# Attention output: gate parts made during the heads, gate products one group ahead, norm by pairs on ScalarE

## The chip, the cores and the metric

The kernel runs on 1 core of one Trainium2 chip. The metric is the device time of one execution in microseconds (us), and the comparison goes by the median of several runs. Engines: PE (TensorE, with its weight load PEld), DVE (VectorE), ACT (ScalarE), POOL (GpSimd) and SP (SyncE, which here only issues DMAs). Each engine has its own instruction stream and the streams meet by semaphores alone.

## What is computed

Two layers, each of an attention-like mixer and a feed-forward part, over x of 8 x 256 tokens with 512 features (2048 tokens). The change lies in the last part of the second mixer ("L1_xattn"); cut to it:

```python
O  = einsum('hst,bthe->bshe', A, V).reshape(b, s, dim)      # the D heads, four of them
mu = O.mean(-1);  var = O.var(-1)
Y  = (O - mu) / sqrt(var + 1e-3) * gn_gamma + gn_beta
W  = relu(x @ wg_w)                                          # x: layer norm of the stream
x  = x + (W * Y) @ wo_w
# next: h = layernorm(x), router and LoRA parts, 44 chunks of the second feed-forward part
```

All of it is in float32, made of float32r parts: a matrix is cut into a high part (a copy in fp32r) and a low part (the matrix minus that copy), and a product is three matmuls: high x high, low x high, high x low (helper `product`, L313 to L317).

## The kernel before

Everything is written out by hand: one function for each engine with its instructions in order, and `wait_ge` on semaphores. The 2048 tokens are 16 tiles of 128, in 4 groups of 4. The eight PSUM banks hold 512 float32 columns each.

**The D heads.** `heads` (L324) runs four heads in the order second(h), first(h+1), weigh(h). On PE, first projects two token groups of the context, second makes the scores and projects the other two, and weigh multiplies the floored scores A with V (24 matmuls of 512 columns). POOL makes the low parts of the context, `low(h, q)` (L529 to L532, tile ccl), in a loop; the projection of group q waits for them. DVE makes |A| (L1565), its floor at 1 (L1567), the low parts of x (xxl, L1541) and of A (al, L1571), and copies half of the results out (ret, L1612). ACT makes the high parts (cch, xxh, ah) and copies the other half (L780). The arrays ct (context) and xt (x, turned so that features lie on partitions) stay in SBUF for the whole stage.

**The output stage.** When all heads are done (`END_D`), `gated` (L349) runs over the four groups: `turned_and_gate(0)`, then `turned_and_gate(g)` and `out_rows(g-1)` in a loop of two, then the rest. For a group:
- DVE: statistics of four tiles (`ln_stats`, L286 to L294), POOL the power -0.5 (L551), DVE applies the norm to four tiles (xn, L299).
- PE turns the four tiles of xn into banks 0 to 3 (L310), ACT scales and shifts them into zt (L804, 16 instructions).
- ACT and POOL make the parts of x of this group, xeh (L789) and xel (L559, one instruction of 2048 columns); PE makes the gate product x @ Wg in banks 4 to 7 (48 matmuls of 512 columns); DVE takes the relu out of PSUM and multiplies it into zt (L1642).
- ACT and DVE cut zt into uh (L821) and ul (L1634); PE multiplies by Wo into banks 0 to 3 (48 matmuls), DVE adds the result to xres (L1656).

The weights' parts wgh, wgl, woh, wol are made once at the start of this stage: high parts on ACT (L793, L796), low parts on DVE (L1627, L1629). The norm of the feed-forward part then goes by pairs of tiles: `pair(n)` on DVE (L1390 to L1398), `pair_root(n)` on POOL (L525, L527), `apply(n)` on ACT (L669), `turn_f` on PE. The last `out_rows` is interleaved with it.

**SP** loads wgf and wof behind the last low part of the context (L403, L404), five small tensors behind `END_D` (L406 to L409), and the first two chunk weights `wst` when the weights' low parts are made (L413).

Of the kernel before, what the change touches and what calls it, by code (L numbers as in the profile page):

```python
# [53 lines left out]
def build(nc, x, ctx_in, taps, d_heads, consts, bits, rw, rb, ew, eb, wh, decay, wg, wo, gb,  # L54
# [15 lines left out]
    with stack:  # L70
# [21 lines left out]
        def place(spot, *buffers):  # L92
# [60 lines left out]
        wgf, wof, wgh, wgl, woh, wol, xeh, xel = place(  # L153
            CT_AT, ("wgf", [P, KB, DIM], F32), ("wof", [P, KB, DIM], F32), ("wgh", [P, KB, DIM], F32R),
            ("wgl", [P, KB, DIM], F32R), ("woh", [P, KB, DIM], F32R), ("wol", [P, KB, DIM], F32R),
            ("xeh", [P, KB, GTOK], F32R), ("xel", [P, KB, GTOK], F32R))
        zt, uh, ul, gbc = place(
            W_AT + 1024, ("zt", [P, KB, GTOK], F32), ("uh", [P, KB, GTOK], F32R), ("ul", [P, KB, GTOK], F32R),
            ("gbc", [P, 2 * KB], F32))

# [31 lines left out]

        def turned(t, tile):
            return t[:, :].rearrange("p (k n) -> p k n", k=KB)[:, :, bass.ts(tile, P)]
# [19 lines left out]
        ln = {st: {k: sem(f"{st}_{k}", 1 if k == "xn" else 0) for k in ("stats", "var", "rstd", "xn")} for st in "AE"}  # L214
# [32 lines left out]
        wg_in, wo_in, wE_high, wE_ready = sem("wg_in"), sem("wo_in"), sem("wE_high"), sem("wE_ready")  # L247
        xeh_ready, xel_ready, wt_done = sem("xeh_ready"), sem("xel_ready"), sem("wt_done", 1)
        y_turned, zt_ready, zu_ready, uh_ready = sem("y_turned", GROUP), sem("zt_ready"), sem("zu_ready", 1), sem("uh_ready")
        ul_ready, wo_done, x3_ready = sem("ul_ready", 1), sem("wo_done", GROUP), sem("x3_ready", GROUP)  # L250
# [89 lines left out]
        END_E = [(x3_ready, TILES)]  # L340
# [5 lines left out]

        EARLY = 1

        def gated(eng, start, turned_and_gate, out_rows):  # L349

            start()
            turned_and_gate(0, True)
            with eng.Fori(1, GROUPS - 1, 1) as g:
                turned_and_gate(g, True)
                out_rows(g - 1)
            turned_and_gate(GROUPS - 1, False)
            out_rows(GROUPS - 2)
            out_rows(GROUPS - 1)
# [13 lines left out]
        def _(sp):  # L372
# [42 lines left out]
            sp.wait_ge(wE_ready, 2)  # L415
# [58 lines left out]
        def _(pool):  # L474
# [74 lines left out]
            def rstd_e(g):  # L549
                pool.wait_ge(ln["E"]["var"], g + 1)  # L550
                pool.tensor_tensor(rstd[:, :], vare[:, 0, :], mhalf[:, :], ALU.pow).then_inc(ln["E"]["rstd"], 1)  # L551

            def nothing(g):
                pass

            def low_xe(g):
                pool.wait_ge(xeh_ready, g + 1)
                pool.sem_inc(passed, 1)
                pool.tensor_tensor(xel[:, :, :], turned_group(xt, g), f(xeh[:, :, :]), ALU.subtract)\  # L559
                    .then_inc(xel_ready, 1)  # L560

            def start():
                rstd_e(0)
                low_xe(0)

            def prepare(g, more):
                if more:
                    rstd_e(g + 1)
                    low_xe(g + 1)

            gated(pool, start, prepare, nothing)
# [4 lines left out]
            for n in range(TILES, TILES + TILES // 2):  # L576
                pair_root(n)
# [24 lines left out]
        def _(act):  # L602
# [59 lines left out]
            def apply(n):  # L662

                act.wait_ge(pair_rstd, n + 1)
                for i in (2 * n, 2 * n + 1):
                    j = i % GROUP
                    if i >= GROUP:
                        act.wait_ge(xn_turned, i - GROUP + 1)
                    act.activation(xn[:, j, :], xres[:, i % TILES, :], ACT.Identity,  # L669
                                   bias=nmr[:, j:j + 1], scale=rstd[:, j:j + 1]).then_inc(xn_ready, 1)  # L670
# [101 lines left out]

            def weigh(h):
# [10 lines left out]
            after(act, END_D)  # L784

            def high_x(g):
                act.wait_ge(wt_done, raised(wt_done) + KB * g)
                act.sem_inc(passed, 1)
                act.activation(xeh[:, :, :], turned_group(xt, g), ACT.Copy).then_inc(xeh_ready, 1)  # L789

            def start():
                act.wait_ge(wg_in, 16)
                act.activation(wgh[:, :, :], wgf[:, :, :], ACT.Copy).then_inc(wE_high, 1)  # L793
                high_x(0)
                act.wait_ge(wo_in, 32)
                act.activation(woh[:, :, :], wof[:, :, :], ACT.Copy).then_inc(wE_high, 1)  # L796

# [1093 lines left out]
```

## Time and profile before

| | |
|---|---|
| runs | 1153.96, 1159.79, 1159.83 us, median 1159.79 |
| the profiled execution | 1154.15 us, span 1152.3 us |
| mean granted clock of TensorE | 0.972 of full |
| busy: PE, PEld, DVE, ACT, POOL | 93%, 75%, 54%, 38%, 51% |

A profile is one execution. Its page gives busy shares and the chain of work that ended last. The views of the trace cut the span into stretches (busy time of each engine and the clock that TensorE was granted, 1.00 being 2.4 GHz and 0.50 being 1.2 GHz) or list instructions in order of time, each with its start and duration and, in brackets, the idle time of its engine just ahead of it and what ended that. Equal instructions in a row are merged ("x4"). A matmul's duration holds its way through the array, so matmuls that follow each other overlap; the distance of their starts is what counts. The D heads run from about 342 to 431 us, the output stage from there to about 549.

### The profile page before, as it was taken

What the parts mean: (1) busy time and instruction counts of PE and PEld (TensorE: products, weight loads), DVE (VectorE), ACT (ScalarE), POOL (GpSimd) and SP (SyncE); (2) the same over time, 40 slices, a digit from 0 to 9 for tenths busy, and PEclk for the clock granted to TensorE, in tenths of its full rate; (3) what the DMA queues carried; (4) which work ended last, traced back from release to release, by engine and by line L of the source; (5) the groups of instructions that cost most, each with busy time, mean ns of one, the idle gap of its engine ahead of it and who ended that gap; (6) DMA issues with size and microseconds to landing.
All of it is one profiled execution on the core that took longest, in us unless ns stands there. A gap on an engine that the chain in (4) does not pass through costs nothing.

```text
span 1152.3 us, 13470 instructions
## 1 busy us (share of the span) xinstructions
PE 1068.2 (93%) x4924; PEld 863.7 (75%) x4924; DVE 624.1 (54%) x1046; ACT 440.6 (38%) x803; POOL 588.8 (51%) x402
## 2 busy tenths in 40 slices
PE   5799998588889985999999999999999999999997
PEld 4577776465568864778668888888888888888886
DVE  6399999846875637756552352423424244242223
ACT  5354444441184535443532332333332232233222
POOL 1588996120032203230227676766776677667662
PEclk9899999888999988999999999999999999999999
DMA  8222121000010012000322212252323432232211
GB/s 306 92 55 64 56 56 28 1 1 1 1 37 1 1 74 97 1 1 1 165 89 87 96 69 87 78 185 105 116 74 107 155 132 80 95 113 87 71 67 37
DMA packets 24560, 85.47 MB, mean 74 GB/s; under 512 B 3169, under 2 KB 3825, under 8 KB 23729
## 3 DMA queue, kind: packets, MB, share of 16 engines
q1 hardware_dynamic: 22384, 80.45, 20.6%
q10 hardware_dynamic: 2112, 4.19, 1.0%
q8 instruction: 38, 0.62, 0.2%
q14 instruction: 26, 0.20, 0.1%
HBM read 74.85 MB, written 9.78 MB: 73 GB/s over the span
## 4 chain that ended last, share of the span: by engine, by line
PE 73%; DVE 19%; issue 4%; ACT 2%; POOL 1%; POOLq 0%; DVEq 0%; ACTq 0%
PE banks L315 23%; PE banks L316 22%; PE banks L317 22%; DVE qt L1372 6%; DVE pr L1366 6%; PE banks L310 3%; DVE pr L1368 1%; DVE stat L1390 1%; DVE junk L1466 1%; PE banks L939 1%; ACT xn L669 1%; PE banks L993 1%; PE banks L1187 0%; DVE xn L299 0%; DVE xtl L1402 0%
## 5 line engine op out<-in xcount | busy, mean ns | idle before, releaser
L1774 DVE TENSOR_TENSOR hf<-banks,silu 128x512 f32<-128x512 f32 x132 | 91.3, 692 | 323.5 <-PE banks L317 322.2
L582 POOL TENSOR_TENSOR gul<-wst,guh 128x1280 fp32r<-128x1280 f32 x44 | 129.9, 2952 | 141.7 <-DVE guh L1672 135.8
L592 POOL TENSOR_TENSOR hl<-hf,hh 128x512 fp32r<-128x512 f32 x129 | 178.2, 1412 | 8.6 <-ACT hh L897 8.6
L939 PE MATMUL banks<-kv,strip 128*128 128x288 f32 x640 | 158.4, 412 | 4.1 <-POOL kv L491 4.1
L897 ACT ACTIVATE hh<-hf 128x512 fp32r<-128x512 f32 x132 | 83.6, 633 | 190.0 <-DVE hf L1774 190.0
L939 PEld LDWEIGHTS banks<-kv,strip 128*128 128x128 f32 x640 | 123.4, 193 | 39.0 <-issue 4.4
L895 ACT ACTIVATE silu<-banks 128x512 f32<-128x512 f32 x132 | 78.9, 598 | 167.4 <-PE banks L317 167.2
L315 PE MATMUL banks<-xf,guh 128*128 128x512 f32 x352 | 137.2, 390 | 0.8 <-POOL gul L582 0.8
L316 PE MATMUL banks<-xf,guh 128*128 128x512 f32 x352 | 137.0, 389 | 0.0
L317 PE MATMUL banks<-xf,gul 128*128 128x512 f32 x352 | 136.9, 389 | 0.0
L525 POOL TENSOR_TENSOR rstd<-vare,mhalf 128x2 f32<-128x2 f32 x24 | 20.2, 842 | 150.7 <-DVE vare L1398 150.7
L587 POOL TENSOR_TENSOR dnl<-wst,dnh 128x640 fp32r<-128x640 f32 x44 | 68.9, 1566 | 42.6 <-DVE dnh L1769 42.6
L315 PEld LDWEIGHTS banks<-xf,guh 128*128 128x128 f32 x352 | 66.1, 188 | 15.8 <-POOL gul L582 1.3
L317 PEld LDWEIGHTS banks<-xf,gul 128*128 128x128 f32 x352 | 66.1, 188 | 13.7
L316 PEld LDWEIGHTS banks<-xf,guh 128*128 128x128 f32 x352 | 66.1, 188 | 13.5
L1366 DVE TENSOR_TENSOR pr<-banks,qx 128x1024 f32<-128x1024 f32 x32 | 65.2, 2038 | 16.5 <-ACT yx L643 15.8
L1372 DVE TENSOR_REDUCE qt<-pr 128x256 f32<-128x2048 f32 x32 | 73.2, 2286 | 1.1
L502 POOL TENSOR_TENSOR pr<-yx,qx 128x768 f32<-128x768 f32 x32 | 59.7, 1866 | 27.0 <-ACT yx L643 21.0
L310 PE MATMUL banks<-cst,xn 128*128 128x128 f32 x320 | 50.0, 304 | 24.9 <-DVE xn L299 12.3
L315 PE MATMUL banks<-rhl,guh 128*128 128x512 f32 x176 | 68.7, 390 | 0.4 <-ACT silu L895 0.3
L315 PE MATMUL banks<-dnh,hh 128*128 128x512 f32 x176 | 68.8, 391 | 0.0
L317 PE MATMUL banks<-rhl,gul 128*128 128x512 f32 x176 | 68.5, 389 | 0.0
(281 smaller groups left out, 2284.3 us busy)
## 6 DMA issues: line engine op xcount, KB each, us to landing
wst<-in_chunk_w SPq DMA_DIRECT2D x44, 960.0 KB, 4.7
strip<-toep SPq DMA_DIRECT2D x32, 256.0 KB, 3.2
xres<-in_x ACTq DMA_DIRECT2D x4, 1024.0 KB, 13.1
cin<-in_ctx SPq DMA_DIRECT2D x16, 256.0 KB, 5.7
xf_s<-xf SPq DMA_DIRECT2D x2, 2048.0 KB, 6.3
out<-xres SPq DMA_DIRECT2D x16, 256.0 KB, 2.1
xf<-xf_s SPq DMA_DIRECT2D x8, 512.0 KB, 5.9
mk<-hot_s SPq DMA_DIRECT2D x14, 256.0 KB
```

What stands on the lines that cost most here:

```text
L310: i = pe.transpose(banks[:, bank, k * P:(k + 1) * P], src[:, k, :], ident)
L315: pe.matmul(dst, wh_, mh_, start=first, stop=False, skip_group_check=check)
L316: pe.matmul(dst, wh_, ml_, start=False, stop=False, skip_group_check=check)
L317: return pe.matmul(dst, wl_, mh_, start=False, stop=last, skip_group_check=check)
L582: pool.tensor_tensor(gul[:, u, :], wst[:, u, 0:GU_W], f(guh[:, u, :]), ALU.subtract).then_inc(gul_ready, 1)
L592: pool.tensor_tensor(hl[:, u, s, :], hf[:, s, :], f(hh[:, u, s, :]), ALU.subtract)\
L895: act.activation(silu[:, s % 2, :], banks[:, 6, :], ACT.Silu).then_inc(silu_done, 1)
L897: act.activation(hh[:, u, s, :], hf[:, s, :], ACT.Copy).then_inc(hh_ready, 1)
L939: mm = pe.matmul(dst, strip[:, h % 3, far:far + P], view(kv, h % 3, m * BATCH * PAIRS, [[PAIRS, BATCH], [1, PAIRS]]), start=m == 0, stop=m ...
L1366: dve.tensor_tensor(view(pr, u, 0, [[HD * HD, MB], [1, 4], [HD, HD]]), rows, view(qx, u, 0, [[2 * HD, MB], [1, 4], [1, HD]]), ALU.mult)
L1372: dve.tensor_reduce(head_cols(qt, h), view(pr, u, 0, [[HD * HD, MB], [HD, HD], [1, HD]]), X_AXIS, ALU.add).then_inc(conv_out, 1)
L1774: dve.tensor_tensor(hf[:, s, :], banks[:, 7, :], silu[:, s % 2, :], ALU.mult).then_inc(mul_done, 1)
```

## The change

- **Weights' parts.** Wg is loaded once ct's first head is used. POOL copies it to wgh in four pieces in head 2 and subtracts to wgl in four pieces in head 3. Wo's high part is made by ACT in four pieces, its low part by POOL in four pieces, one behind each of the first four `pair_root`. Its load wof now lies on zt's place, and the first scaling waits for its low parts.
- **x parts.** They are made in pieces of 512 columns, `high_xe(g, k)` on ACT and `low_xe(g, k)` on POOL. Group 0's are made in the heads, groups 1 and 2 around the last weigh, group 3 behind the second scaling. The low parts overwrite xt.
- **Gate products.** PE runs gate(0) ahead of the last weigh, and then gate(1), turn(0), gate(2), turn(1), out(0), gate(3), turn(2), out(1), turn(3), out(2), out(3). ACT copies each gate bank to SBUF (`keep_w`, 16 copies), so DVE's relu and product read SBUF twice.
- **Norm.** The group norm of Y goes by pairs like the norm that follows (pair indices move up by 8): statistics on DVE, roots and -mean x root on POOL, application on ACT.
- The loops are written out. The first chunk weights are loaded behind the first low part of xf.

The core of the diff:

```diff
+        def xel(g, k):
+            return xtr[:, k * TOKENS + g * GTOK:k * TOKENS + (g + 1) * GTOK]
...
-            sp.wait_ge(ccl_ready, 4 * RHEADS)
+            sp.wait_ge(ccl_ready, 4)
             sp.dma_start(wgf[:, :, :], wg).then_inc(wg_in, 16)
+            for u in range(2):
+                sp.wait_ge(sc_done[u], raised(sc_done[u]) + 2 * RHEADS)
             sp.dma_start(wof[:, :, :], wo).then_inc(wo_in, 16)
             after(sp, END_D)
-            sp.dma_start(gbc[:, :], gb).then_inc(wo_in, 16)
+            sp.dma_start(gbc[:, :], gb).then_inc(lw_in, 16)
...
-            sp.wait_ge(wE_ready, 2)
+            sp.wait_ge(xfl_ready, 1)
             load(0, 0, 0)
...
-            with pool.Fori(1, RHEADS, 1) as h:
-                for q in range(4):
-                    low(h, q)
-            after(pool, END_D)
...
+            def low_xe(g, k):
+                pool.wait_ge(xeh_ready, KB * g + k + 1)
+                pool.wait_ge(xxl_ready, 4 * k + g + 1)
+                pool.tensor_tensor(xel(g, k), xt_part(g, k), f(xe[g][:, k, :]), ALU.subtract).then_inc(xel_ready, 1)
+
+            for h in range(1, RHEADS):
+                low(h, 0)
+                low(h, 1)
+                if h == 1:
+                    low_xe(0, 0)
+                if h == 2:
+                    pool.wait_ge(wg_in, 16)
+                    for k in range(KB):
+                        pool.tensor_copy(wgh[:, k, :], wgf[:, k, :]).then_inc(wgh_ready, 1)
+                    low_xe(0, 1)
+                if h == 3:
+                    for k in range(KB):
+                        pool.wait_ge(wgh_ready, k + 1)
+                        pool.tensor_tensor(wgl[:, k, :], wgf[:, k, :], f(wgh[:, k, :]), ALU.subtract).then_inc(wgl_ready, 1)
+                    low_xe(0, 2)
+                low(h, 2)
+                low(h, 3)
+            low_xe(0, 3)
+            for g in (1, 2):
+                for k in range(KB):
+                    low_xe(g, k)
+            for n in range(TILES, TILES + TILES // 2):
+                pair_root(n)
+                if n < TILES + KB:
+                    k = n - TILES
+                    pool.wait_ge(woh_ready, k + 1)
+                    pool.tensor_tensor(wol[:, k, :], wof[:, k, :], f(woh[:, k, :]), ALU.subtract).then_inc(wol_ready, 1)
+                if n == TILES + KB + 1:
+                    for k in range(KB):
+                        low_xe(3, k)
...
+            def keep_w(g, jb):
+                act.wait_ge(wt_done, KB * g + jb + 1)
+                if g >= 2:
+                    act.wait_ge(zu_ready, KB * (g - 2) + KB)
+                act.activation(wk[g % 2][:, jb, :], banks[:, W_BANKS[g][jb], :], ACT.Copy).then_inc(wr_ready, 1)
+
             def weigh(h):
                 if h == RHEADS - 1:
+                    act.wait_ge(mv_done[0], raised(mv_done[0]) + 2 * RHEADS)
+                    act.wait_ge(mv_done[1], raised(mv_done[1]) + 2 * RHEADS)
+                    for k in range(KB):
+                        high_xe(1, k)
                     act.wait_ge(a_ready, h + 1)
                     act.activation(ah[:, :], aw[:, :], ACT.Copy).then_inc(ah_ready, 1)
+                    for k in range(KB):
+                        high_xe(2, k)
+                    for jb in range(KB):
+                        keep_w(0, jb)
...
+                if h < 2:
+                    if h == 0:
+                        act.wait_ge(xn_turned, 2 * TILES)
+                    high_xe(0, 2 * h)
+                    high_xe(0, 2 * h + 1)
...
+            def scaled(g):
+
+                if g == 0:
+                    act.wait_ge(wol_ready, KB)
+                    act.wait_ge(lw_in, 80)
+                else:
+                    act.wait_ge(ul_ready, GROUP * g)
...
+            apply(TILES)
+            keep_w(1, 0)
+            apply(TILES + 1)
+            keep_w(1, 1)
+            keep_w(1, 2)
+            keep_w(1, 3)
+            scaled(0)
+            apply(TILES + 2)
+            keep_w(2, 0)
+            apply(TILES + 3)
+            keep_w(2, 1)
+            high_u(0)
+            keep_w(2, 2)
+            keep_w(2, 3)
+            scaled(1)
+            apply(TILES + 4)
+            apply(TILES + 5)
+            for k in range(KB):
+                high_xe(3, k)
...
+            high_u(1)
+            for jb in range(KB):
+                keep_w(3, jb)
+            scaled(2)
+            apply(TILES + 6)
+            apply(TILES + 7)
+            high_u(2)
+            scaled(3)
+            high_u(3)
...
+            def weigh_last(h):
+                if h == RHEADS - 1:
+                    gate(0)
+                weigh(h)
+
+            heads(pe, start, first, second, weigh_last)
...
+            gate(1)
+            turn_y(0)
+            gate(2)
+            turn_y(1)
+            out_rows(0)
+            gate(3)
+            turn_y(2)
+            out_rows(1)
+            turn_y(3)
+            out_rows(2)
+            out_rows(3)
...
+            def gated_features(g):
+                for jb in range(KB):
+                    dve.wait_ge(wr_ready, KB * g + jb + 1)
+                    dve.wait_ge(zt_ready, GROUP * g + GROUP)
+                    dve.scalar_tensor_tensor(zt[:, jb, :], wk[g % 2][:, jb, :], 0.0, zt[:, jb, :], ALU.max, ALU.mult)\
+                        .then_inc(zu_ready, 1)
...
+            for n in range(4):
+                pair(TILES + n)
+            gated_features(0)
+            for j in range(GROUP):
+                low_u(0, j)
+            pair(TILES + 4)
+            pair(TILES + 5)
+            gated_features(1)
+            out_rows(0)
+            pair(TILES + 6)
+            pair(TILES + 7)
+            gated_features(2)
+            out_rows(1)
+            gated_features(3)
+            out_rows(2)
+            out_rows(3)
```

## Rows read from the trace of the kernel before

**Rows 1.** The page: busy time by engine (us, share, instructions), and the chain's shares.

```profile
PE 1068.2 (93%) x4924; PEld 863.7 (75%) x4924; DVE 624.1 (54%) x1046; ACT 440.6 (38%) x803; POOL 588.8 (51%) x402
PE 73%; DVE 19%; issue 4%; ACT 2%; POOL 1%; POOLq 0%; DVEq 0%; ACTq 0%
```

**Rows 2.** Stretches: length, busy (count) PE, PEld, DVE, ACT, POOL, PEclk, DMA, GB/s.

```profile
418.94:523.40 104.46, 84.60 (x375) 69.89 (x375) 67.43 (x95) 44.48 (x87) 26.80 (x10) 0.90 0.08 27
```

**Rows 3.** Timeline, PE, output stage: start, duration, instruction, [idle before, what ended it].

```profile
422.41 0.79 PE L315 MATMUL banks<-vh,ah 128*128 128x512 f32 x1 [3.47 <-DVE al L1571]
...
441.17 3.65 PE L310 MATMUL banks<-cst,xn 128*128 128x128 f32 x16 [10.27 <-DVE xn L299]
...
463.03 0.79 PE L315 MATMUL banks<-xeh,wgh 128*128 128x512 f32 x1 [5.11 <-POOL xel L559]
...
523.86 0.39 PE L315 MATMUL banks<-woh,uh 128*128 128x512 f32 x1
```

**Rows 4.** Timeline, PE: the end of a gate product and a turn.

```profile
455.78 0.39 PE L317 MATMUL banks<-xeh,wgl 128*128 128x512 f32 x1
456.01 1.91 PE L310 MATMUL banks<-cst,xn 128*128 128x128 f32 x16
```

**Rows 5.** Timeline, DVE: the norm's applications of groups 0 and 1.

```profile
436.31 6.09 DVE L299 TENSOR_SCALAR xn<-ret,mom,rstd 128x512 f32<-128x512 f32 x4 [1.22 <-POOL rstd L551]
...
451.04 1.92 DVE L299 TENSOR_SCALAR xn<-ret,mom,rstd 128x512 f32<-128x512 f32 x4 [1.12 <-POOL rstd L551]
```

**Rows 6.** Timeline, DVE and ACT: prices of a pair, a copy, a scaling, a cast.

```profile
536.21 1.28 DVE L1390 BATCH_NORM_STATS2 stat<-xres 128x6 f32<-128x512 f32 x2
...
539.12 1.52 ACT L669 ACTIVATE xn<-xres,nmr,rstd 128x512 f32<-128x512 f32 x2 [3.56 <-POOL nmr L527]
...
429.67 0.60 ACT L780 ACTIVATE ret<-banks 128x512 f32<-128x512 f32 x1 [3.61 <-PE banks L317]
...
442.36 5.69 ACT L804 ACTIVATE zt<-banks,gbc 128x128 f32<-128x128 f32 x16 [5.02 <-PE banks L310]
...
599.76 0.82 DVE L1672 CAST guh<-wst 128x1280 fp32r<-128x1280 f32 x1
```

**Rows 7.** Landing time of the wgf load; timeline, DVE: first reader of wst.

```profile
DMA to landing us min/median/max: 4.9/4.9/4.9
...
568.39 0.82 DVE L1683 CAST guh<-wst 128x1280 fp32r<-128x1280 f32 x1
```

**Rows 8.** Timeline, POOL, DVE and PE ahead of weigh(2), in the D heads.

```profile
396.67 2.55 POOL L531 TENSOR_TENSOR ccl<-ct,cch 128x512 fp32r<-128x512 f32 x2 [6.88 <-ACT cch L714]
...
399.14 0.69 DVE L1565 SCALAR_TENSOR_TENSOR aw<-aw 128x512 f32<-128x512 f32 x1
...
401.41 0.69 DVE L1571 TENSOR_TENSOR al<-aw,ah 128x512 fp32r<-128x512 f32 x1
...
402.15 0.50 PE L315 MATMUL banks<-vh,ah 128*128 128x512 f32 x1
```

**Rows 9.** Timeline, POOL and PE, head 1: context low parts and their reader.

```profile
366.58 2.53 POOL L531 TENSOR_TENSOR ccl<-ct,cch 128x512 fp32r<-128x512 f32 x2 [8.71 <-ACT cch L714]
...
370.47 0.40 PE L315 MATMUL banks<-cch,grh 128*128 128x512 f32 x1
```

**Rows 10.** Timeline, DVE and POOL: two-input DVE instructions beside POOL's.

```profile
664.42 1.45 DVE L1739 TENSOR_TENSOR rf<-ra,mk 128x512 f32<-128x512 f32 x1
665.80 1.78 DVE L1740 TENSOR_TENSOR rf<-ra,mk 128x512 f32<-128x512 f32 x1
667.50 0.68 DVE L1739 TENSOR_TENSOR rf<-ra,mk 128x512 f32<-128x512 f32 x1
...
665.28 1.74 POOL L592 TENSOR_TENSOR hl<-hf,hh 128x512 fp32r<-128x512 f32 x1
```

**Rows 11.** Stretches as in rows 2: after the 3.47 idle, and a head change.

```profile
422.40:428.40 6.00, 5.99 (x14) 4.73 (x15) 0.35 (x1) 0.60 (x1) 0.00 (x0) 0.50 0.00 0
...
367.00:372.00 5.00, 4.48 (x35) 4.38 (x36) 2.36 (x5) 2.17 (x5) 2.11 (x2) 1.00 0.00 0
```

More of the change, by code:

```diff
@@ L151, in build @@
             ("xxh", [P, 2, GTOK], F32R), ("xxl", [P, 2, GTOK], F32R))
[L153 to L156, printed above, removed]
+        wgf, = place(CT_AT, ("wgf", [P, KB, DIM], F32))
+        wgh, wgl = place(CT_AT + 8192, ("wgh", [P, KB, DIM], F32R), ("wgl", [P, KB, DIM], F32R))
+        wr0, = place(CT_AT, ("wr0", [P, KB, GTOK], F32))
+        wr1, woh, wol, xe1, xe2 = place(
+            CT_AT + 24576, ("wr1", [P, KB, GTOK], F32), ("woh", [P, KB, DIM], F32R), ("wol", [P, KB, DIM], F32R),
+            ("xe1", [P, KB, GTOK], F32R), ("xe2", [P, KB, GTOK], F32R))
+        xe0, = place(BASE + 34816, ("xe0", [P, KB, GTOK], F32R))
+        wof, = place(W_AT + 1024, ("wof", [P, KB, DIM], F32))
         zt, uh, ul, gbc = place(
@@ L781, in weigh @@
                                    banks[:, bank, :].rearrange("p (b e) -> p b e", b=4), ACT.Copy).then_inc(ro_act, 1)
-            heads(act, start, first, second, weigh)
[L784 to L796, printed above, removed]
-            def scaled(g, more):
-                act.wait_ge(ul_ready, raised(ul_ready) + GROUP * g)
+                if h < 2:
[3 more added lines that the diff above has]
+                    high_xe(0, 2 * h + 1)
+            heads(act, start, first, second, weigh)
+            act.wait_ge(ao_done, raised(ao_done) + 4 * RHEADS)
+            act.wait_ge(wo_in, 16)
+            for k in range(KB):
+                act.activation(woh[:, k, :], wof[:, k, :], ACT.Copy).then_inc(woh_ready, 1)
+            def scaled(g):
[4 more added lines that the diff above has]
+                    act.wait_ge(ul_ready, GROUP * g)
                 for j in range(GROUP):
-                    act.wait_ge(y_turned, raised(y_turned) + GROUP * g + j + 1)
+                    act.wait_ge(xn_turned, 2 * TILES + GROUP * g + j + 1)
                     for k in range(KB):
@@ L827, in _ @@
-            gated(act, start, scaled, out_rows)
+            apply(TILES)
[15 more added lines that the diff above has]
+            apply(TILES + 5)
@@ L857, in _ @@
             keep_a(0, 0)
-            apply(TILES + 5)
+            apply(TILES + 13)
             high_f(8)
@@ L1132, in weigh, with gate @@
                     mm.then_inc(ao_done, 1)
-            heads(pe, start, first, second, weigh)
-            after(pe, END_D)
-            def turned_and_gate(g, more):
+            def gate(g):
+                pe.wait_ge(wgl_ready, KB)
+                pe.wait_ge(xel_ready, KB * g + KB)
+                for jb in range(KB):
+                    if g == 0 and jb >= 2:
+                        pe.wait_ge(vl_ready[jb - 2], raised(vl_ready[jb - 2]) + 2 * RHEADS)
+                    if g == 1 and jb == 1:
+                        pe.wait_ge(ro_act, raised(ro_act) + 2 * RHEADS)
+                        pe.wait_ge(ro_vec, raised(ro_vec) + 2 * RHEADS)
+                    if g >= 2:
+                        pe.wait_ge(wr_ready, KB * (g - 1) + jb + 1)
+                    for k in range(KB):
+                        mm = product(pe, banks[:, W_BANKS[g][jb], :], wgh[:, k, jb * P:(jb + 1) * P],
+                                     wgl[:, k, jb * P:(jb + 1) * P], xe[g][:, k, :], xel(g, k), k == 0, k == KB - 1)
+                    mm.then_inc(wt_done, 1)
@@ L1672, in cut_gu @@
                 dve.tensor_copy(guh[:, u, :], wst[:, u, 0:GU_W]).then_inc(guh_ready, 1)
-            gated(dve, start, gated_features, out_rows)
+            for n in range(4):
[14 more added lines that the diff above has]
+            out_rows(3)
             for n in range(4, TILES // 2):
-                pair(TILES + n)
+                pair(TILES + 8 + n)
                 low_f(2 * n - 4)
```

168 lines of the change are left out of this document (61 added, 107 removed).

## The prediction

> **What bounds the kernel now.** I read the page's busy times and chain first: PE is busy for 93% of the span and the chain that ended last is 73% PE [rows 1]. So the kernel is a TensorE kernel, and a change to helpers is worth only what PE idle time or half-clock time it removes. The stretch table then shows where that time is [rows 2]: from the end of the D heads' scores (418.94, 3.47 ahead of the matmul at 422.41) to the first out-projection matmul of group 2 (523.86 [rows 3]) PE is busy 84.6 us of 104.5 and its granted clock is 0.90. The work in this stretch, at full clock: a 512-column matmul comes every 0.227 us (455.78 to 456.01, rounded) and 16 transposes take 1.91, the last overlapping what follows, 1.75 from start to start [rows 4]. Weigh of the last head is 24 matmuls (5.4 us), four gate products are 192 (43.5), two out-projections are 96 (21.8), four turns are 7.0: 77.7 us. The stretch is 104.9, so **27.2 us** are idle or slow. They are, in order [rows 3]: 3.5 idle before weigh(3) and then 24 matmuls until 430.9, 8.3 instead of 5.4 (2.9 more); 10.3 idle before the first turn of Y, and that turn in 3.5 instead of 1.75 with a slow start of the gate (2.3 in all); 5.1 idle until xel of group 1 exists, then 1.3 at half clock; the last 1.8 are waits of some tenths. What ends the 10.3 is a chain of DVE and POOL work: statistics of four tiles, the POOL power, and four xn applies that took 6.09 us where four later ones took 1.92, because POOL's xel ran beside them [rows 5].
>
> **Gain in the output stage.** (Times below are those of before, as if the D heads kept their time.)
> 1. gate(0) moves in front of weigh(3): its inputs (Wg parts, x parts of group 0) are made in the D heads. PE runs it from 418.94 to 429.8, weigh(3) to 435.3, gate(1) to 446.2, turn_y(0) to 448.1, gate(2) to 459.0, turn_y(1) to 460.9, all without a pause if ACT keeps up. The old cover of DVE's floor(3) was none; it is now 10.9 us.
> 2. The norm by pairs: pair(16) starts when the last ret copy is through, 436.4. A pair takes 2.9 us from its first statistic to ACT's start, of which I put 1.8 on DVE and 1.0 on POOL, and 1.5 on ACT for two tiles [rows 6]. POOL does a wol piece (1.27) behind each of four roots, and pair n+2 waits for apply n. The wol pieces end at 440.6, 442.9, 445.2 and 447.5.
> 3. **The wait added**: scaled(0) waits for all four wol pieces, since zt lies on wof: it starts at 447.5, not at its first turned tile. Queued behind it on ACT are two applies, four keeps of the gate, four uh copies and scaled(1). With 5.69 for a scaled, 1.52 for an apply of two, 0.6 for a keep or a uh [rows 6], scaled(1) starts at 447.5 + 5.7 + 1.5 + 0.6 + 1.5 + 0.6 + 2.4 + 1.2 = 461.0 and gives its first tile at 462.4. PE waits for it with out_rows(0) from 460.9: 1.5 us. POOL's pieces can push DVE's small pair instructions and so this chain by some 1 more: 2.5.
> 4. Group 3's x parts: high_xe(3) comes behind scaled(1) and two applies, POOL needs 4 x 1.27 for them, so they are complete 14.4 us after scaled(1) starts; PE is through out_rows(0) 12.4 after it. Stall 2.0 to 2.6, taken as 2.3. Before out_rows(1) and out_rows(2) PE waits for the first tile of scaled(2) and (3): 0.5 and 1.0.
> 5. Sum of stalls left: 6.3, and one spell at half clock, 1.7 (about as after the 5.1 gap). **27.2 - 8.0 = 19.2 us** gained in this stage. Bounds: 22 without contention and slow spells; 14 with every POOL piece in the way once and two slow spells.
> The two spare moves cost nothing. SP's wof load now waits for the last scores; it is issued near 419, the equal load of wgf lands in 4.9 us [rows 7], and woh needs it at 434. Nothing stands behind it on SP until the heads end. The five small loads behind it are issued 4.5 us later than now and are needed at 447.5. The first wst loads move behind the first xf part, near 535; their first reader stands at 568.39 [rows 7], so over 20 us of cover remain. The tail from out_rows(3) on is the same work in the same order.
>
> **Cost in the D heads.** POOL gets 4 copies of Wg and one low_xe in the middle of head 2, 4 subtractions and one low_xe in head 3. All lie in POOL's queue behind low(h,1) and ahead of low(h,2), and start the moment low(h,1) ends: 399.22 in the old times of head 3 [rows 8]. POOL has 8.7 us of idle time before low(h,2) [rows 9], so low(h,2) isn't late; nor is head 1, where the two ACT copies and low_xe(0,0) make ccl 1.3 + 1.3 late against 370.47, the first project that reads it (366.58 + 1.3 now, 369.2 then [rows 9]). But look what DVE does in those 5 us [rows 8]: |A|, floor, two xxl, and al, and al ends at 402.10 where weigh starts at 402.15. There is no slack. DVE instructions that read two SBUF tensors, and the copies and scalings from SBUF to SBUF, do not run beside a POOL tensor instruction in this trace: the xn applies lost 4.2 us to xel [rows 5]; two rf in a row, each 0.68 alone, took 1.45 and 1.78 beside two hl of POOL, and the second of these (665.28, 1.74 instead of 1.29) let the first rf through and then held up the second [rows 10]. So they take turns, even when DVE's instructions stand back to back. |A| is in when POOL starts (399.14); then floor, xxl, xxl and al each wait for one POOL piece: **al is late by four pieces**, and weigh with it. In head 3 a piece is a subtraction, 1.26: 5.0 us. In head 2 it is a one-input copy that no row of POOL shows. High end: the two-input row, 1.26, so 5.0. Low end: DVE's own one-input cast takes 0.82 for 1280 columns and its two-input subtraction 0.69 for 512 [rows 6, 8], half per column, so 0.65 and 2.6. I take the low end, as the nearest in kind. Sum 7.6, at most 10.0; nothing if the claims don't collide at all.
> The clock: the gap of 3.5 at 418.94 was followed by 5.7 us at 0.50; the gap of 1.0 at every head change leaves 1.00 [rows 11]. Half clock costs half of its time. A gap of 5.0 should bring 1.7 to 3.4, one of 2.6 brings 0 to 3.4: I take 3.4 together. **Cost 11.0 us.**
> The Trainium skill, "SBUF — State Buffer", section "SBUF: two separate sides", says that DVE and GpSimd share a port pair as an exclusive lock held for the whole instruction, for DVE instructions with two SBUF inputs or in a two-port mode. The rf rows agree; by that rule ACT's applies, which the change puts in the place of DVE's, never wait. "GPSIMD Engine Reference", section 4.1, calls one-input work on GpSimd roughly line rate; that would make the copy about 0.45 and the estimate for head 2 1.8 instead of 2.6. No run here shows it.
>
> **Sum.** 19.2 - 11.0 = 8.2 us. Against the profiled execution: its time is 1154.15 (span 1152.3), so 1146.0. The runs shown are 1153.96, 1159.79 and 1159.83; the profiled one is of the lower kind, 5.6 under the median, and 8.2 off the median is 1151.6. I forecast 1149, between the two.
>
> **Rivals.**
> *The port claims don't matter in the heads* (POOL's pieces slip into the holes, or PE's own queue hides al). For it: POOL is 8 us idle there. Against: al ends 0.05 ahead of weigh, and the rf rows. Then 19.2 are kept: 1135 on the profile's basis, 1140 on the median's. Chance 0.17.
> *A draw*: copies at 1.26 each, slow clock after both gaps (3.4 each), output stage at its low end: 14 - 10.0 - 6.8 = -2.8; with one of the slow spells missing it is +0.6. For it: POOL rows are all at 1.26 for this shape. 1153 to 1162. Chance 0.24.
> *Slower*: |A| loses the tie with POOL's first piece (it starts 0.08 ahead of low(h,1)'s end now) so al waits for five pieces in both heads: 12.6, clock 6.8; and low_xe(3) and wol, made in the output stage, hold gated and ul there. These now read SBUF on both sides, where gated read PSUM, so each of the 8 in a POOL burst can lose 1.3. This costs 10 beyond the stalls above: 19.2 - 19.4 - 10 = -10. With the fifth piece and both slow spells in place, the sign turns at the first held instruction, and 0.5% is passed at the fifth. 1164 to 1170. Chance 0.09.
> *It doesn't do what it says* (gate(0) starts late, since Wg's low parts come last on POOL): against, they are issued 15 us ahead of 418.94. It is in the draw's chance.
>
> **How the numbers follow.** Main forecast 0.50. Within it the gain runs from about 2 to 14 us. A measurement of this kernel can tell about 0.5% (5.8 us) from no change. Faster by more: three quarters of the main case plus nearly the whole first rival, and a little of it lost to which kind of run the median falls on: 0.56. Within 0.5%: the rest of the main case and most of the draw: 0.31. Slower: the third rival and a part of the draw: 0.13. The range goes from the first rival on the profile's basis to the draw's upper part: 1136 to 1161.
>
> **What would show it.** PE without a gap at 418.94 and clock 1.00 there; turn_y(0) right behind gate(1). In heads 2 and 3 a PE gap of 2.6 and of 5.0 ahead of weigh(1) and weigh(2), al late, DVE's xxl at 1.3 to 1.9 instead of 0.69 and POOL pieces stretched by 0.4 to 0.6. POOL's Wg copies at 0.65, not 1.3. ACT's scaled(0) starting where the fourth wol ends. The forecast is wrong if PE runs through weigh(1) and weigh(2) as now, or if gated and ul in the output stage take over 1 us each.

## The result, and the profile after

Nine runs of each kernel on one chip: before 1152.72 us (1151.57 to 1159.83), after **1145.81 us** (1145.11 to 1148.22), ratio after to before 0.9934, with a 95% interval of 0.9915 to 0.9953. So the change gains 6.9 us, 0.6%; the forecast was 1149, from a sum of 8.2. The profiled execution after is the 1145.11 one.

The page: busy time by engine, and the shares of the chain [rows 1 for before].

```profile
span 1143.3 us, 13422 instructions
...
PE 1065.9 (93%) x4924; PEld 861.4 (75%) x4924; DVE 607.7 (53%) x1040; ACT 459.1 (40%) x849; POOL 608.9 (53%) x438
...
PE 71%; DVE 20%; issue 4%; ACT 3%; POOL 1%; POOLq 0%; DVEq 0%; ACTq 0%
```

The shares hardly move: work went from DVE to ACT and POOL, and PE is still the bound. What moved shows in two places.

**The output stage.** Stretches (length, busy of PE, PEld, DVE, ACT, POOL, PEclk, DMA, GB/s) from the end of the scores of head 3 to the first out-projection of group 2, then right behind PE's two long gaps in the D heads [rows 2, 11 for before]:

```profile
426.85:511.64 84.79, 78.58 (x377) 65.17 (x376) 41.42 (x86) 54.95 (x114) 30.09 (x33) 1.00 0.07 22
...
381.50:385.50 4.00, 4.00 (x12) 3.15 (x12) 0.76 (x2) 0.60 (x1) 0.00 (x0) 0.63 0.00 0
409.00:412.50 3.50, 3.50 (x11) 2.71 (x11) 0.73 (x2) 0.60 (x1) 0.00 (x0) 0.60 0.00 0
```

104.9 us have become 84.8, **20.1 less** (forecast 19.2), and the clock in them is 1.00. PE is busy 78.6 of the 84.8; the prediction counted 77.7 of work. The rest, 6.2, is what PE waits for. PE's waits from 374 to 535 us (total, times, longest):

```profile
PE banks L330 <- DVE al L1651: 7.5, 2, 5.1
PE banks L330 <- ACT zt L834: 4.3, 3, 2.6
PE banks L330 <- DVE ret L1692: 2.0, 2, 1.0
PE banks L330 <- issue: 1.9, 1, 1.9
PE banks L325 <- DVE xf L1727: 0.2, 1, 0.2
```

The second and fourth lines are the stage's four stalls: 4.3 + 1.9 = 6.2. The fourth is put down to "issue", but it ends with the parts of x of group 3: POOL's last piece of them ends at 483.99, PE's gate(3) starts at 484.09.

**The D heads.** The first line is new: PE waits for the low part of A twice, 7.5 us. Here is head 3, the timeline of DVE, POOL and PE (start, duration, instruction, idle before and what ended it) [rows 8 for before]:

```profile
399.62 0.69 DVE L1642 TENSOR_TENSOR aw<-banks,dmask 128x512 f32<-128x512 f32 x1 [1.72 <-PE banks L332]
400.34 1.75 DVE L1645 SCALAR_TENSOR_TENSOR aw<-aw 128x512 f32<-128x512 f32 x1
402.13 1.39 DVE L1647 TENSOR_SCALAR aw<-aw 128x512 f32<-128x512 f32 x1
403.44 3.42 DVE L1621 TENSOR_TENSOR xxl<-xt,xxh 128x512 fp32r<-128x512 f32 x2
406.78 1.74 DVE L1651 TENSOR_TENSOR al<-aw,ah 128x512 fp32r<-128x512 f32 x1
```

```profile
400.27 6.04 POOL L567 TENSOR_TENSOR wgl<-wgf,wgh 128x512 fp32r<-128x512 f32 x4
406.27 1.70 POOL L552 TENSOR_TENSOR xtr<-xt,xe 128x512 fp32r<-128x512 f32 x1
```

```profile
408.58 0.80 PE L330 MATMUL banks<-vh,ah 128*128 128x512 f32 x1 [5.09 <-DVE al L1651]
```

Five POOL pieces and five DVE instructions go through each other, one of the one, one of the other: each xxl takes 1.7 instead of 0.64, POOL's piece 1.5 instead of 1.26. al is late and PE stands for 5.09 us. From the last ret copy of one head to that of the next there are 20.7 us in an undisturbed head; head 2 has 24.8 and head 3 27.4 (+4.1, +6.7 = **10.8**, forecast 11.0).

**The account.** The profiled spans differ by 9.0. Of that 3.0 is there before head 2: POOL's last ccl of head 1 starts at 375.99 before and at 372.97 after. The change did little there that could help; such offsets of 1 to 3 us come and go between all the kernels below, with the places of PE's half-clock spells in the 370 us ahead. What follows that instruction I call **the tail**: it is the cleanest part of a profile to compare. Before 776.3, after 770.3, 6.0 less: about 20.1 won in the stage, 10.8 lost in the heads, and 3.1 lost in two half-clock spells of after, from 555 and from 1135 on, which before does not have. Each lasts 3.4 us. What one costs is read by taking the same matmul, counted from the end of the program, in both profiles: after falls back by 1.6 over the first spell and by 1.5 over the second. Both come behind a wait of PE that before has as well, at full clock (1.53 us before the first, 2.77 before the second).

### The profile page after: what moved, and what is told of

Read it like the earlier page. It is cut to its first block, busy times and chain, and to the rows that moved or that the text cites. A ratio compares the mean times of both kernels' runs of the same rounds, so it can differ in the third digit from the quotient of the medians.

```text
span 1143.3 us, 13422 instructions
## 1 busy us (share of the span) xinstructions
PE 1065.9 (93%) x4924; PEld 861.4 (75%) x4924; DVE 607.7 (53%) x1040; ACT 459.1 (40%) x849; POOL 608.9 (53%) x438
## 4 chain that ended last, share of the span: by engine, by line
PE 71%; DVE 20%; issue 4%; ACT 3%; POOL 1%; POOLq 0%; DVEq 0%; ACTq 0%
PE banks L330 22%; PE banks L331 21%; PE banks L332 21%; DVE qt L1450 6%; DVE pr L1444 6%; PE banks L325 2%; DVE pr L1446 1%; DVE stat L1469 1%; ACT xn L682 1%; DVE junk L1546 1%; ACT zt L834 1%; PE banks L1265 1%; PE banks L989 1%; PE banks L1043 1%; DVE xxl L1621 0%
## 5 line engine op out<-in xcount | busy, mean ns | idle before, releaser
L529 POOL TENSOR_TENSOR rstd<-vare,mhalf 128x2 f32<-128x2 f32 x32 | 25.8, 806 | 184.1 <-DVE vare L1478 184.1
L332 PEld LDWEIGHTS banks<-xf,gul 128*128 128x128 f32 x352 | 66.1, 188 | 13.8
L330 PE MATMUL banks<-rhl,guh 128*128 128x512 f32 x176 | 68.8, 391 | 0.4 <-ACT silu L945 0.3
L331 PE MATMUL banks<-rhl,guh 128*128 128x512 f32 x176 | 68.6, 390 | 0.0
L332 PE MATMUL banks<-dnh,hl 128*128 128x512 f32 x176 | 68.5, 389 | 0.0
```

Of the source, the lines that this page charges most:

```text
L330: pe.matmul(dst, wh_, mh_, start=first, stop=False, skip_group_check=check)
L331: pe.matmul(dst, wh_, ml_, start=False, stop=False, skip_group_check=check)
L332: return pe.matmul(dst, wl_, mh_, start=False, stop=last, skip_group_check=check)
```

## The experiments

Two theories stood against each other. **Turns**: POOL's pieces and DVE's chain to al hold each other up, and the whole cost of the heads goes if the pieces come behind al. **Load**: the heads cost because POOL, ACT and DVE have more to do in them, wherever the pieces stand. All ratios are against runs of the kernel before on the same chip. Its medians in these groups lie between 1152.65 and 1153.06, so medians of different groups can be set side by side to within some tenths. Tails are of the profiled executions.

| kernel | median us | ratio, 95% interval | tail us |
|---|---|---|---|
| e1_behind_al | 1132.19 | 0.9819 [0.9803, 0.9835] | 756.5 |
| e2_head2_only | 1140.30 | 0.9887 [0.9869, 0.9905] | 763.6 |
| e3_before_pieces | 1162.34 | 1.0076 [1.0058, 1.0095] | 786.8 |
| e7_before_pieces_al | 1152.86 | 0.9999 [0.9990, 1.0009] | 776.6 |
| e4_gate0_late | 1149.43 | 0.9978 [0.9965, 0.9991] | 773.8 |
| e9_al_gate0 | 1139.36 | 0.9876 [0.9853, 0.9899] | 763.3 |
| e5_act_order | 1132.72 | 0.9825 [0.9801, 0.9848] | 757.0 |
| e6_apply_dve | 1133.67 | 0.9827 [0.9804, 0.9851] | 756.9 |
| e8_he_first | 1133.48 | 0.9825 [0.9802, 0.9848] | 756.3 |
| e10_uh_early | 1129.24 | 0.9787 [0.9772, 0.9802] | 753.1 |

### The pieces behind al, in both heads and in one

```diff
                 if h == 2:
+                    pool.wait_ge(al_ready, raised(al_ready) + h)
                     pool.wait_ge(wg_in, 16)
...
                 if h == 3:
+                    pool.wait_ge(al_ready, raised(al_ready) + h)
```

> The changed kernel (1145.8 us median), but in heads 2 and 3 POOL waits for al of the head before ahead of its Wg copies, Wg subtractions and low_xe. Nothing else moves. Theory (turns at the port between DVE and POOL): al is back in time, the PE gaps of 2.43 and 5.09 us ahead of weigh(1) and weigh(2) go, and the slow spells behind them (1.7 and 1.6 us) with them: 10.8 us less, about 1135. POOL has 5 pieces of 0.65 to 1.3 us and 5.8 us until the next low part, so that may be late by under 1 us, hidden by 2.5 us until its reader. Rival (the gaps come from something else that the change brought into the heads, such as ACT's extra copies): no change, 1144 to 1147.

Measured 1132.19, 13.6 under the changed kernel; the tail is 13.8 shorter, for 10.8 of the heads and 3.1 of the two late spells, which e1 does not have. DVE, POOL of e1 in head 2:

```profile
378.56 1.28 DVE L1623 TENSOR_TENSOR xxl<-xt,xxh 128x512 fp32r<-128x512 f32 x2
379.76 0.68 DVE L1653 TENSOR_TENSOR al<-aw,ah 128x512 fp32r<-128x512 f32 x1
```

```profile
380.51 2.29 POOL L563 CAST wgh<-wgf 128x512 fp32r<-128x512 f32 x4 [3.05 <-DVE al L1653]
382.76 1.29 POOL L552 TENSOR_TENSOR xtr<-xt,xe 128x512 fp32r<-128x512 f32 x1
```

Each xxl is back at 0.64 and al at 0.68, PE has no wait for al in either head, and the pieces still end in time: the very same work, started 3.1 us later. The load theory falls. The copy by itself is seen here: 2.29 for four, 0.57 each.

e2_head2_only has the first of the two waits alone.

> As the run before it, but only head 2's pieces wait for al; head 3's stay where the change put them. Theory: 4.1 us less than the changed kernel (gap 2.43 and 1.7 of half clock), about 1141.7; head 3 keeps its gap of 5.09. Rival (the cost is that of any POOL burst of this length, or the clock alone): the difference is not in the proportion of 4.1 to 6.7.

1140.30; PE waits for al once, 5.1. The step from e2 to e1 (head 3) is 8.1, in the tails 7.1; the stretch of head 3 in the changed kernel had said 6.7, and 0.4 more is lost there in e2, since less of its half-clock spell lies under PE's gap. From after to e2 (head 2) it is 5.5, in the tails 6.7, of which 4.1 are the head and 3.1 the two late half-clock spells, absent here too, less the same 0.4. Why they are gone was not tried.

### The pieces put into the kernel before

Ten POOL instructions of the same shape, on ct and into the idle xn, behind low(2,1) and low(3,1) of the kernel before, which has none of the rest of the change.

```diff
+            for h in range(1, RHEADS):
+                low(h, 0)
+                low(h, 1)
+                if h > 1:
+                    for i in range(4):
+                        piece(h == 2)
+                    piece(False)
+                low(h, 2)
+                low(h, 3)
```

> The kernel before, and only POOL work added: four copies of 128x512 and one subtraction behind low(2,1), four subtractions and one more behind low(3,1), all into the tile of xn, which is free in the heads; nobody reads them. It prices the cost in the heads by itself. Theory: 10.8 us slower than before, 1163.5 on a median of 1152.7, with gaps of 2.4 and 5.1 us ahead of weigh(1) and weigh(2). Rival (the gaps in the changed kernel come from its waits and ACT copies): no slower.

1162.34, +9.6 on the median of before beside it; the tail is 10.5 longer, PE waits for al twice, 2.21 and 3.94. The second was expected at 5.1. These subtractions read the same tensor twice and take 1.04 alone (in e7), not 1.26, and each link of DVE's chain is late by 0.83 to 0.85 at a piece, where the changed kernel has 1.06; the floor is late by 0.72. In head 3 of this kernel (timeline of DVE):

```profile
403.99 2.97 DVE L1563 TENSOR_TENSOR xxl<-xt,xxh 128x512 fp32r<-128x512 f32 x2
406.88 1.52 DVE L1593 TENSOR_TENSOR al<-aw,ah 128x512 fp32r<-128x512 f32 x1
```

e7_before_pieces_al is the same with one more line, `pool.wait_ge(al_ready, raised(al_ready) + h)`, ahead of the pieces.

> The same ten POOL pieces in the kernel before, but each burst waits for al of the head before. Theory: the same POOL work costs nothing there, 1152 to 1154: what costs is where it stands against DVE's chain. Rival (POOL's work in itself is the price, by delaying its own low parts): 2 to 10 us slower.

1152.86, ratio 0.9999, tail 0.3 longer: the same ten instructions cost nothing behind al. POOL's five subtractions of head 3, alone here:

```profile
400.91 5.04 POOL L556 TENSOR_TENSOR xn<-ct 128x512 f32<-128x512 f32 x5 [3.06 <-DVE al L1595]
```

With e1 this settles the heads from both sides: it is the place, not the work.

### gate(0) in front of the last weigh

```diff
             def weigh_last(h):
+                weigh(h)
                 if h == RHEADS - 1:
                     gate(0)
-                weigh(h)
```

with ACT's `keep_w(0, *)` behind woh.

> The changed kernel (1145.8) with one part undone: gate(0) stands behind weigh(3) on PE instead of ahead of it (and its four copies on ACT behind the last ret copies). Theory (gate(0) is the cover of DVE's and ACT's work on A of the last head): PE stands idle from the last scores to al, 5.5 us in the changed kernel's times, and then runs at half clock for 3.4 to 6.8 us; 7.2 to 8.9 us slower, 1153 to 1155. Rival (the norm's chain is what had to be covered, and two gates behind weigh cover it just as well): within 1 us of the changed kernel, since gate(0) and gate(1) are then both behind the last ret copies.

1149.43, only 3.6 over the changed kernel, where 7 to 9 were expected. PE does wait (5.4 once more for al, and half clock behind it), yet the profile of e4 lacks the two late spells of after. The rows say 5.4 + 1.9 (half clock, by e9 below) - 0.7 (waits for zt of 3.6 instead of 4.3) = 6.6; less 3.1 for the two spells is 3.5, and the tails say 3.5. So the same edit was tried on e1, which has no late spells to lose.

> e1_behind_al with gate(0) behind weigh(3) instead of in front, and its four keep copies on ScalarE behind woh: the same edit as in e4_gate0_late, on a kernel whose D heads lose nothing. Theory (gate(0) in front covers floor(3) to al(3) on DVE, a PE gap of 5.4 us in e4_gate0_late at the end of the scores, with a half-clock spell behind it of 1.7 to 3.4 lost, and 4.5 of that is won back since the statistics of Y start earlier in front of gate(1) and PE's waits for scaled are shorter by 0.7): slower than e1_behind_al by 5 to 8, so 1137 to 1140. Rival (the place of gate(0) is worth only what e4_gate0_late showed against the changed kernel, 3.6 us, whatever the heads do): 1135 to 1136.5. The trace should show one PE wait for al of about 5.4 at the end of the scores and half clock behind it.

1139.36, **7.2** over e1, tails 6.8. PE's gap in e9, the stretch behind it, and what DVE does ahead of it:

```profile
423.11 0.80 PE L330 MATMUL banks<-vh,ah 128*128 128x512 f32 x1 [5.45 <-DVE al L1653]
```

```profile
423.20:427.50 4.30, 4.30 (x11) 3.42 (x12) 0.00 (x0) 1.81 (x4) 4.30 (x4) 0.56 0.00 0
```

```profile
418.54 1.73 DVE L1647 SCALAR_TENSOR_TENSOR aw<-aw 128x512 f32<-128x512 f32 x1
420.30 1.37 DVE L1649 TENSOR_SCALAR aw<-aw 128x512 f32<-128x512 f32 x1
422.36 0.69 DVE L1653 TENSOR_TENSOR al<-aw,ah 128x512 fp32r<-128x512 f32 x1 [0.69 <-ACT ah L804]
```

4.3 us at 0.56 cost 1.9. The gap is 5.45 where before had 3.47 [rows 3]: |A| and the floor meet POOL's parts of x group 1 and take 1.73 and 1.37 instead of 0.69 and 0.43, together 1.98 more, which is the difference. The new POOL work collides here too, but gate(0) hides it. Its place is worth a third of the stage's 20.1. How the rest divides among the parts of the change (weights and x parts made early, norm by pairs, gates a group ahead) was not tried; the trace shows only that PE's gaps of 10.27 and 5.11 [rows 3] are gone with them.

### The two stalls of the output stage

In e1 they are these (timeline of PE):

```profile
462.13 0.47 PE L330 MATMUL banks<-woh,uh 128*128 128x512 f32 x1 [2.58 <-ACT zt L836]
...
475.16 0.47 PE L330 MATMUL banks<-xe,wgh 128*128 128x512 f32 x1 [1.86 <-issue]
```

e5_act_order takes ACT work out of the way of both, on top of e1:

```diff
             high_u(0)
+            scaled(1)
             keep_w(2, 2)
             keep_w(2, 3)
-            scaled(1)
-            apply(TILES + 4)
-            apply(TILES + 5)
             for k in range(KB):
                 high_xe(3, k)
+            apply(TILES + 4)
+            apply(TILES + 5)
```

> The changed kernel with POOL's pieces behind al (1132.2) and two steps of ACT's order moved: scaled(1) comes ahead of keep_w(2,2) and (2,3), and high_xe(3) ahead of the applies of pairs 20 and 21. Theory (ACT's queue is what PE waits for with out_rows(0), and what makes x parts of group 3 late): the wait of 2.6 us becomes 1.5 and that of 1.9 goes, 3.0 us less: 1129.2. Rival (PE waits for POOL or DVE there, and ACT's order only moves the wait): no change, 1131 to 1133.

1132.72: **no gain**, a miss. The 1.86 is gone, the 2.58 is not. ACT of e5:

```profile
456.10 2.19 ACT L846 ACTIVATE uh<-zt 128x512 fp32r<-128x512 f32 x4
459.30 5.69 ACT L836 ACTIVATE zt<-banks,gbc 128x128 f32<-128x128 f32 x16 [1.01 <-DVE ul L1710]
```

scaled(1) now stands for 1.01 and waits for DVE's last ul: zt is one buffer, and the two keeps I had moved (1.07 in after) were covered by ul anyway. And two half-clock spells of 3.4 us came up, one right behind the 2.58 gap and one at 543. The same gap stays at full clock in e1 (stretch behind it, first e1, then e5):

```profile
463.00:466.40 3.40, 3.40 (x17) 2.78 (x16) 0.99 (x6) 3.40 (x11) 1.08 (x3) 1.00 0.00 0
```

```profile
461.30:464.60 3.30, 3.30 (x10) 2.61 (x10) 1.38 (x6) 3.30 (x11) 1.57 (x4) 0.61 0.00 0
543.20:546.50 3.30, 3.30 (x14) 1.97 (x13) 1.89 (x3) 1.70 (x3) 0.00 (x0) 0.61 0.00 0
```

e8_he_first has the lower swap alone (high_xe(3) ahead of the applies).

> e1_behind_al with one swap on ScalarE: the four x copies of group 3 (high_xe(3)) in front of the norm's applies 20 and 21; scaled(1) and the four keeps stay where they are. In e1_behind_al PE waits 1.9 us once in front of gate(3) (idle time put to issue) and 2.6 us in front of out_rows(0). Theory (the x parts of group 3 come late because two applies of 0.7 us each stand ahead of them): the 1.9 shrinks to about 0.5, the 2.6 stays, the time is 1130.5 to 1131.5 where e1_behind_al took 1132.2. Rival (the saved wait is given back, as in e5_act_order, since turn_y(2) then waits for the applies, or a spell at half clock appears behind the 2.6 wait): 1132 to 1134, and PE shows waits for xn or a half-clock spell between 440 and 550 that e1_behind_al does not have.

1133.48. The rival came out: the 1.86 is gone from the waits, and one half-clock spell of 3.4 us from 543.9 on (1.6 lost) takes it back; the tail is 0.2 under e1's. This also gives the account of e5. Matmul by matmul against e1, e5 falls back by 1.4 over its first spell, wins 2.0 where the wait for x parts was, and falls back by 1.3 over the second spell: +0.5 with the small rest, as the tails say. Both spells of e5 begin inside a wait of PE (at 460.4 and 542.4), so part of each costs nothing. Which gap draws a spell can't be told beforehand from these rows.

e6_apply_dve gives the norm's application back to DVE, where ACT had it (8 tensor_scalar pairs behind their `pair_rstd`), on top of e5.

> As the run before it, but Y's norm by pairs is applied on DVE (tensor_scalar with mean and root, as the kernel before did it) instead of on ACT. Theory: ACT's chain from scaled(0) to scaled(1) loses two applies (3.0 us), of which the wait for zt's product in keep_w(2,0) takes some back; the wait at out_rows(0) shrinks from 1.5 to about 0.3, and DVE's applies, which hold the shared port, cost POOL's wol pieces 0.3 to 0.5 each: 0 to 1 us less than 1129.2. Rival (DVE's applies held by POOL as in the kernel before, up to 1.3 each): 2 to 4 us slower than the run before it, and the move to ACT is then worth something by itself.

1133.67, tail 756.9 against 757.0: no difference. Neither forecast came: the wait at out_rows(0) is still 2.53, where the theory had 0.3, and the time is not 2 to 4 us longer. ACT isn't the bound of this stage by its load.

e10_uh_early then shortens the chain that e5's ACT line points at: gated(0), uh, ul, scaled(1).

```diff
             scaled(0)
             apply(TILES + 2)
-            keep_w(2, 0)
             apply(TILES + 3)
-            keep_w(2, 1)
+            keep_w(2, 0)
             high_u(0)
+            keep_w(2, 1)
             scaled(1)
```

> e5_act_order with ScalarE's order behind scaled(0) changed: apply(18), apply(19), keep_w(2,0), high_u(0), keep_w(2,1), scaled(1) instead of apply(18), keep_w(2,0), apply(19), keep_w(2,1), high_u(0), scaled(1). In e5_act_order gated(0) on VectorE ends near 453.7, ScalarE's first uh copy starts at 456.10 behind two applies (the two stand in one group of 1.51 with a keep on each side), the last ul ends at 459.27 and scaled(1) starts at 459.30 [1.01 <-DVE ul]; out_rows(0) waits 2.58 us for it. Theory (the wait at out_rows(0) is the chain scaled(0), gated(0), uh(0), ul(0), scaled(1), since zt is one buffer; the two keeps behind high_u that e5_act_order moved away were covered by ul): scaled(1) starts about 1.7 us earlier, 457.6, the wait falls from 2.58 to about 0.9, the time is 1.7 under e5_act_order (1132.7), so 1130.5 to 1131.5, and some tenths less if no half-clock spell follows the shorter wait (down to 1129). Rival (turn_y(1) or the first tile of scaled(1) itself is the bound): the wait stays above 2, the time 1132 to 1134, and scaled(1) starts no earlier.

**1129.24**, 3.5 under e5 and 2.0% under before, the best kernel here. ACT and PE of e10:

```profile
451.43 3.00 ACT L684 ACTIVATE xn<-ret,nmr,rstd 128x512 f32<-128x512 f32 x4
454.33 0.60 ACT L795 ACTIVATE wr<-banks 128x512 f32<-128x512 f32 x1
454.82 2.18 ACT L846 ACTIVATE uh<-zt 128x512 fp32r<-128x512 f32 x4
456.90 0.58 ACT L795 ACTIVATE wr<-banks 128x512 f32<-128x512 f32 x1
458.01 5.69 ACT L836 ACTIVATE zt<-banks,gbc 128x128 f32<-128x128 f32 x16 [0.52 <-DVE ul L1710]
```

```profile
459.66 0.47 PE L330 MATMUL banks<-woh,uh 128*128 128x512 f32 x1 [0.69 <-ACT zt L836]
```

Both applies now lie in the time in which ACT used to stand waiting for DVE's gated product; uh and scaled(1) start 1.3 earlier than in e5 (1.9, since e10 stands 0.6 later at the common instant), and PE's wait falls by as much, from 2.58 to 0.69 (forecast 0.9): the chain is the right one. PE's waits for zt are 2.5 in all instead of 4.3, the one for x parts 0.4 instead of 1.9: 3.3, and the tail is 3.4 under e1's. No spell follows. Against e5 the step is twice the forecast 1.7, 3.9 in the tails: 1.9 are the wait and 2.7 the two spells of e5, less 0.4 for the wait for x parts, which comes back, and some tenths. For spells that go the theory had allowed "some tenths".

## Why the prediction was right, and where not

*The cost in the heads: right, in place, mechanism and size.* Forecast: 2.6 and 5.0 late in heads 2 and 3, and 3.4 for the clock. Measured: PE waits 2.43 and 5.09, and 3.3 for the rest (10.8 - 7.5). e1 and e7 take it away by place alone. But the sums inside were made up otherwise. Forecast: four holds, each as long as its piece. In head 3 there are five, since |A| is held too (1.75 instead of 0.69), and each is shorter than its piece: 1.06, 0.96, 1.07, 1.07 and 1.06 against e1's durations, 5.2 in all for pieces of 1.26. In head 2 the timeline of DVE is:

```profile
375.54 1.07 DVE L1645 SCALAR_TENSOR_TENSOR aw<-aw 128x512 f32<-128x512 f32 x1
376.65 0.72 DVE L1647 TENSOR_SCALAR aw<-aw 128x512 f32<-128x512 f32 x1
377.29 2.11 DVE L1621 TENSOR_TENSOR xxl<-xt,xxh 128x512 fp32r<-128x512 f32 x2
379.32 1.74 DVE L1651 TENSOR_TENSOR al<-aw,ah 128x512 fp32r<-128x512 f32 x1
```

The four copies hold for 0.38, 0.29, 0.42 and 0.42, and al meets the fifth piece, the subtraction low_xe, for 1.06: 2.6 in all. 4 x 0.65 was the right total by two errors, a fifth piece left out and each hold taken too long.

*The copy.* Taken at 0.65, bounds 0.65 to 1.26; it is 0.57 alone (e1) and 0.85 while it takes turns with DVE (3.39 for four in the changed kernel). The low end was the right end, and lay 0.08 too high. The estimate from "GPSIMD Engine Reference" of the Trainium skill, section 4.1, was 0.45; the row is nearer to the estimate from DVE's rows.

*The turns.* The rows of head 3 show turn and turn about even when both engines have their next instruction ready. xxl at 1.3 to 1.9 was forecast and is 1.7; POOL's pieces were to be stretched by 0.4 to 0.6 and are stretched by 0.25 (1.51 for 1.26) and 0.28 (0.85 for 0.57), only the fifth by 0.4. The Trainium skill, "SBUF — State Buffer", section "SBUF: two separate sides", has it that whoever starts first keeps the pair for the whole instruction. The trace agrees as far as each is late by nearly one piece, 1.0 of 1.26 and 0.4 of 0.57; the last 0.2 of a piece is not felt. That ACT never waits for it agrees too (an apply is 0.76 beside POOL's wol and without).

*The stage: 20.1 for 19.2.* The stalls were forecast as 2.5, 2.3, 0.5 and 1.0, 6.3 in all. They are 2.58, 1.86, 0.43 and 1.33: 6.2. Three steps behind that sum were off all the same.
- The chain up to scaled(1) was summed as ACT's own list: 42.1 us behind the end of the scores. It starts 42.6 behind (469.41 - 426.85). But the list alone is not what holds it. ACT of after:

```profile
460.94 1.60 ACT L682 ACTIVATE xn<-ret,nmr,rstd 128x512 f32<-128x512 f32 x2
463.83 0.60 ACT L793 ACTIVATE wr<-banks 128x512 f32<-128x512 f32 x1 [1.29 <-DVE zt L1702]
464.33 1.51 ACT L682 ACTIVATE xn<-ret,nmr,rstd 128x512 f32<-128x512 f32 x2
465.74 0.58 ACT L793 ACTIVATE wr<-banks 128x512 f32<-128x512 f32 x1
466.21 2.19 ACT L844 ACTIVATE uh<-zt 128x512 fp32r<-128x512 f32 x4
468.30 1.07 ACT L793 ACTIVATE wr<-banks 128x512 f32<-128x512 f32 x2
469.41 5.69 ACT L834 ACTIVATE zt<-banks,gbc 128x128 f32<-128x128 f32 x16
```

  DVE of after, the ul of group 0:

```profile
466.88 2.50 DVE L1708 TENSOR_TENSOR ul<-zt,uh 128x512 fp32r<-128x512 f32 x4 [3.14 <-ACT uh L844]
```

  The 1.29 at 463.83 is **a wait that the change adds and I did not name**: keep_w(2, 0) writes the buffer that gated(0) reads, so it waits for all four of gated(0), with an apply and the uh copies queued behind it. And ul(0) ends at 469.38, 0.03 ahead of scaled(1): two chains end together, and the sum hit the right number by the one that isn't alone. That part was luck. The price of it was e5, built on the list, which gained nothing; e10 shows the chain that holds.
- One half-clock spell of 1.7 was forecast in the stage. There is none. Against that, PE is busy for 78.6 where 77.7 was counted: three of the four turns took 1.91, not 1.75, and the rest is some tenths in the products. With both, and 0.1 less of stalls, 19.2 becomes 20.1.
- The gated and ul instructions were to be held by POOL only in the "slower" rival. They are hardly held: gated takes 2.50 for four, ul 0.82 and 1.16 once each. What is held are DVE's tiny steps of the norm, a 128x2 tensor_scalar that takes 0.81 instead of 0.17 when it meets a wol piece:

```profile
447.48 0.81 DVE L1476 TENSOR_SCALAR vare<-mom 128x2 f32<-128x2 f32 x1
```

*The spare moves cost nothing*: there is no PE wait for a load in the stage or behind it. Tried by themselves they were not.

*The median.* The forecast of 1149 took the middle between the profiled execution and the median shown. That was the weakest step: over nine runs before stands at 1152.72, beside its profiled execution, and only three of nine were near 1159.7. 1154.15 - 8.2 = 1146.0, the sum itself, is within 0.2 of the measured median, but that is luck. Two things that were not in the sum nearly cancel: 3.0 in favour ahead of the heads, and two late half-clock spells against, 3.1. The tails give a gain of 6.0 and the medians 6.9, where 8.2 was forecast; stage and heads by themselves were each better than forecast, by 0.9 and 0.2.

*The rivals.* "The port claims don't matter in the heads" is refuted by e1 and e3. The draw needed copies at 1.26. "Slower" began as told, |A| lost the tie in both heads and al met five pieces; but five holds were 5.2 and 2.6, not 12.6 together, and gated and all but two of the ul were not held.

## What to carry to other kernels

When work is moved to an engine that is idle, ask what the other engine does in that very hole: here the idle 8 us of POOL lay over the one DVE chain that PE waits for, and ten instructions cost 10.8 us of the 20.1 won, which one wait per head, behind the last link of that chain, gives back. Sum a chain by every buffer that it reuses, not by one engine's list, and look for a second chain that ends in the same instant before taking work off the first. And compare profiles from a common instruction onwards: spells of half clock elsewhere move the total by 2 to 3 us, as much as such an edit is worth.

## What was not expected of the hardware

- A 2.58 us gap of PE was followed by 3.3 us at 0.61 in e5 and by full clock in e1, with the same instructions of PE around it; gaps of 5.09 and 5.45 were always followed by a slow stretch (0.60, 0.56), those of 1.0 in the heads never. A 1.53 us wait was followed by full clock in before, e1 and e10 and by 0.60 in e8.
- POOL and DVE alternate one for one over five instructions in a row; neither gets two turns. A DVE chain is late by the number of its links that meet a POOL piece, times the piece less 0.2: 0.3 to 0.4 for a copy of 0.57, 0.7 to 0.85 for a subtraction of 1.04 (e3 beside e7), 1.0 to 1.1 for one of 1.26.
- Even a 128x2 tensor_scalar on DVE waits for the end of a POOL piece (0.81 for 0.17), while BATCH_NORM_STATS2 beside it is not held (1.29 for two, as without POOL).
